# Cross attention: the probabilities turned by VectorE in 32x32 blocks and moved through DRAM

## Chip, cores and metric

The kernel is one program on 1 core of a Trainium2 chip. Its metric is the device time of one execution in microseconds, as a median of several runs. Engines are named as the profile names them: PE (TensorE), with PEld its weight loads, DVE (VectorE), ACT (ScalarE), POOL (GpSimd), SP (SyncE, which only issues DMAs here).

## The reference

The program computes a block of three layers over 64 sequences of 32 tokens of width 512, each layer added to its input: cross attention to 257 context rows of width 256, self attention, and a layer of experts. The change touches the first.

```python
def _L0_xattn_ref(x, z, Wq, Wkv, Wo):        # x (64, 32, 512) normalised, z (64, 257, 256)
    Q = (x @ Wq.T).reshape(B, xN, 16, 32)
    KV = (z @ Wkv.T).reshape(B, zN, 2, 16, 32)
    K, V = KV[:, :, 0], KV[:, :, 1]
    attn = jax.nn.softmax(jnp.einsum('bqhd,bkhd->bhqk', Q, K) * SCALE, axis=-1)
    O = jnp.einsum('bhqk,bkhd->bqhd', attn, V).reshape(B, xN, 512)
    return O @ Wo.T
```

## The kernel before

**Tiling.** 2048 tokens are 16 token tiles i of 128 tokens, each of which holds four samples (sequences) j of 32 tokens, so there are 64 samples s = 4i + j. The loop runs over pairs of tiles, with the first and the last pair written out. The key and value weights are absorbed: the queries of a tile are multiplied with Wk once (absorb_k), so that a sample's scores are QK times the raw context z, and the probabilities are multiplied with z first (gather_z, result U) and with Wv and Wo once per tile (values, project_o). A precise product is three matmuls in fp32r with operands split in a high and a low part (product, L49 to L54): ACT makes a high part by a cast, DVE the low part by a subtraction.

**One sample.** Rows are (head, token) pairs, in four groups m of 128 rows; columns are the 257 keys. PE makes the scores in four banks bank_s (scores, 24 matmuls), DVE takes two maxima (L696), ACT makes four exponentials into Pr with their sums (L596), DVE scales Pr by the reciprocal sums (L703, L707, L708). Keys 0 to 255 must then be brought onto the partitions for gather_z: PE turns the eight 128x128 blocks of Pr (turn_p, L412) into bank_pt, which are the banks 2 and 3 of bank_s; ACT casts them into PT_hi (L564) and DVE subtracts for PT_lo (L641), both out of PSUM. Key 256 has its own path (p_last, last_weights, last_rows, last_values).

**What prepares the next sample.** PE turns z (turn_z, L385), ACT casts it into zT_hi (L541) and DVE makes zT_lo (L628); ACT casts the sample's slice of QK (L558), DVE makes QK_lo (L633). POOL writes the last key's column (last_key, L742) and splits z, not turned, for gather_z (split_z: a small carrier instruction L748, the cast L749, the subtraction L751). SP loads the raw z of a sample four samples ahead (L142, 256 KB) and per tile eight small pieces for the last key (L355).

**Order.** It is written out by hand per engine, and each engine runs its list in order, with semaphores between them. PE in sample s: scores(s), gather_z(s-1), turn_z(s+1), then what belongs to the tile (absorb_k for j = 0 and 2, values at j = 0, project_o at j = 1, half of project_q at j = 2 and at j = 3), and turn_p(s) last. split_z(s) on POOL waits for the gather_z before it (pe_U), because it overwrites its buffer, and for DVE's QK_lo of the next sample (v_QK, L760).

Of the kernel before, what the change touches and what calls it, by code (L numbers as in the profile page):

```python
# [16 lines left out]
F32 = mybir.dt.float32  # L17
# [6 lines left out]
P = 128  # L24
# [60 lines left out]
def cross_attention(nc, x_in, ctx_in, Wq, Wkv, Wo, x_res, ident, vlast_dram, spare,  # L85
# [21 lines left out]
    with ExitStack() as ctx:  # L107
# [31 lines left out]
        z_got = [sem(f"z_got{j}") for j in range(BT)]  # L139

# [158 lines left out]
        (PT_hi, PT_lo) = held.parts(held.w13[1], 1, 2, C)  # L299
# [5 lines left out]
        OT_hi, OT_lo = held.parts(held.xT, 1, 2, P)  # L305
        carrier = sb("xa_carrier", [P, 1])
# [13 lines left out]
        g_L, g_Zh, g_Z = sem("g_L"), sem("g_Zh"), sem("g_Z")  # L320
# [18 lines left out]
        def step_of(i, u, j, more):  # L339

            if j % 2 == 0 and (more or u == 0):
                return 1 - u, j, 2 * (i + 1) + 2, BT * i + NQ + j + 2
            return None

        with nc.Block() as block:
            @block.sync
            def _(sp):
# [8 lines left out]

                def tile(i, u, first, last, more):
                    for j in range(BT):  # L360
                        s = BT * i + j
                        if not first:
                            sp.wait_ge(pe_T, s - BT + 1)
                            sp.wait_ge(g_Z, s - BT + 1)
                            load_z(sp, s, j)
                    if first:
# [4 lines left out]
                        sp.wait_ge(vl_put, 32)  # L371
                    last_values(i)
                    if first:
                        weights.load(sp)
                by_pair(sp, tile)

            @block.tensor
            def _(pe):
# [29 lines left out]
                def turn_p(s):  # L408
                    pe.wait_ge(v_N, s + 1)
# [11 lines left out]
                def scores(s, some):  # L421
# [3 lines left out]
                    for m in range(NQ):  # L425
                        if some and m >= 2:
                            pe.wait_ge(v_PT, 2 * s + m - 3)
# [5 lines left out]
                def gather_z(s):  # L433

                    pe.wait_ge(g_Z, s + 1)
                    pe.wait_ge(v_PT, 2 * s + 2)
                    need(pe, U_out, s)
                    for k in range(KL):
                        for c in range(CH):
                            mm = product(pe, bank_u[:, k],  # L440
                                         (zn_hi[:, c, k * P:(k + 1) * P], zn_lo[:, c, k * P:(k + 1) * P]),
                                         (PT_hi[:, c, :], PT_lo[:, c, :]), c == 0, c == CH - 1)
                    mm.then_inc(pe_U, 1)

# [7 lines left out]
                def values(i):  # L452

                    pe.wait_ge(U_out, BT * i + BT)
                    for m in range(NQ):
                        for part in range(KL):
                            for hh in range(4):
                                h = 4 * m + hh
                                mm = pe.matmul(bank_o[hh * HD:(hh + 1) * HD, m * P:(m + 1) * P],
                                               WvT[:, part, h * HD:(h + 1) * HD], U[:, part, h, :], start=False,  # L460
# [30 lines left out]
                def tile(i, u, first, last, more):  # L491
                    for j in range(BT):
# [4 lines left out]
                        if j == 0 and not first:  # L497
# [3 lines left out]
                        if first and j == 1:  # L501
# [3 lines left out]
                        if j == 0 and not first:  # L505
                            last_values(i - 1)
                        if j == 2 and not last:
                            need(pe, v_OP, i)
                            turn_x(pe, i + 2)
# [8 lines left out]
                        if j == 0 and not first:  # L518
                            values(i - 1)
                        if j == 1 and not first:  # L520
                            project_o(i - 1)
                        if j == 2 and more:
                            project_q(i + 2, 0)
                        if j == 3 and more:
                            project_q(i + 2, 1)
# [6 lines left out]
                gather_z(s_end - 1)  # L532
# [5 lines left out]
            def _(act):  # L538
# [22 lines left out]
                def pt_hi(s):  # L561
                    for c in range(CH):
                        act.wait_ge(pe_PT, 2 * s + c + 1)
# [1873 lines left out]
```

## Time and profile before

| | us |
|---|---|
| median of 3 runs (1493.66 to 1495.46) | 1495.41 |
| profiled execution, first to last instruction | 1492.9 |
| PE busy | 1434.5 (96%) |
| DVE busy | 1088.6 (73%) |
| ACT busy | 807.5 (54%) |
| POOL busy | 543.6 (36%) |
| TensorE clock granted, mean | 0.990 |

The profiled execution's own time was not kept beside its span; the span is 2.5 us under the median of the runs. In a row of a timeline the first number is the start in us from the span's start, the second the duration. A group of instructions gives their busy time and mean duration in ns, and, behind the bar, how long the engine idled just ahead of them and what ended that. Tile names are shortened by the profile: split and split_xT are parts of held buffers, xa_s is bank_s, xa_u the banks of gather_z, xa_z the bank of turn_z.

### The profile page before, as it was taken

What the parts mean: (1) busy time and instruction counts of PE and PEld (TensorE: products, weight loads), DVE (VectorE), ACT (ScalarE), POOL (GpSimd) and SP (SyncE); (2) the same over time, 40 slices, a digit from 0 to 9 for tenths busy, and PEclk for the clock granted to TensorE, in tenths of its full rate; (3) what the DMA queues carried; (4) which work ended last, traced back from release to release, by engine and by line L of the source; (5) the groups of instructions that cost most, each with busy time, mean ns of one, the idle gap of its engine ahead of it and who ended that gap; (6) DMA issues with size and microseconds to landing.
All of it is one profiled execution on the core that took longest, in us unless ns stands there. A gap on an engine that the chain in (4) does not pass through costs nothing. (4 is left out here: it accounts for less than half of the span.)

```text
span 1492.9 us, 39481 instructions
## 1 busy us (share of the span) xinstructions
PE 1434.5 (96%) x14944; PEld 1281.3 (86%) x14944; DVE 1088.6 (73%) x1945; ACT 807.5 (54%) x1525; POOL 543.6 (36%) x810
## 2 busy tenths in 40 slices
PE   7999999999999999998999998799999999999998
PEld 6888888988888888887778786698999999999997
DVE  3676777767777677776667686797887878787785
ACT  4666666666666666654434434345555545555452
POOL 1222222221222222224866876453333333333232
PEclk9999999999999999999999999899999999999999
DMA  6301101000001100100011014179877878787871
GB/s 239 125 28 31 30 22 29 29 22 29 22 28 28 29 28 23 30 9 1 31 38 38 32 38 155 57 220 314 281 263 247 286 253 267 262 279 238 292 256 44
DMA packets 130734, 174.11 MB, mean 117 GB/s; under 512 B 16953, under 2 KB 89337, under 8 KB 130626
## 3 DMA queue, kind: packets, MB, share of 16 engines
q1 hardware_dynamic: 120242, 145.56, 30.1%
q0 software_dynamic: 10384, 27.05, 5.0%
q8 instruction: 75, 1.23, 0.4%
q14 instruction: 33, 0.27, 0.1%
HBM read 157.18 MB, written 19.06 MB: 118 GB/s over the span
## 5 line engine op out<-in xcount | busy, mean ns | idle before, releaser
L2229 DVE TENSOR_TENSOR split<-raw,split 128x1024 fp32r<-128x1024 f32 x204 | 242.3, 1220 | 7.2 <-ACT split L2169 6.0
L52 PE MATMUL bank<-split_xT,split 128*128 128x256 f32 x768 | 216.5, 282 | 0.4 <-DVE split L2229 0.2
L54 PE MATMUL bank<-split_xT,split 128*128 128x256 f32 x768 | 215.4, 281 | 0.0
L53 PE MATMUL bank<-split_xT,split 128*128 128x256 f32 x768 | 215.4, 280 | 0.0
L2169 ACT CAST split<-raw 128x1024 fp32r<-128x1024 f32 x202 | 203.2, 1048 | 6.9 <-DMA raw<-in_L_ffn_W_dram 3.2
L596 ACT ACTIVATE Pr<-xa_s,nmax 128x257 f32<-128x257 f32 x256 | 118.7, 473 | 124.9 <-DVE nmax L696 124.8
L2189 ACT ACTIVATE sl<-bank 128x256 f32<-128x256 f32 x115 | 44.2, 384 | 240.8 <-PE bank L54 223.5
L52 PE MATMUL xa_s<-split,split 128*128 128x258 f32 x512 | 150.5, 294 | 1.9 <-DVE split L628 1.9
L52 PEld LDWEIGHTS bank<-split_xT,split 128*128 128x128 f32 x768 | 144.9, 189 | 7.0 <-issue 2.8
L53 PEld LDWEIGHTS bank<-split_xT,split 128*128 128x128 f32 x768 | 145.0, 189 | 3.1
L53 PE MATMUL xa_s<-split,split 128*128 128x258 f32 x512 | 145.6, 284 | 0.0
L54 PE MATMUL xa_s<-split,split 128*128 128x258 f32 x512 | 145.2, 284 | 0.0
L54 PEld LDWEIGHTS bank<-split_xT,split 128*128 128x128 f32 x768 | 144.8, 189 | 0.0
L641 DVE TENSOR_TENSOR split<-xa_s,split 128x512 fp32r<-128x512 f32 x128 | 82.6, 686 | 81.4 <-ACT split L564 80.1
L2313 POOL TENSOR_TENSOR e_carrier<-count 128x1 f32<-128x1 f32 x84 | 29.3, 349 | 306.8 <-DMA of_row<-slot_val 102.8
L748 POOL TENSOR_TENSOR xa_carrier<-mhalf 128x1 f32<-128x1 f32 x64 | 12.6, 197 | 285.2 <-DVE split L633 280.6
L696 DVE TENSOR_REDUCE nmax<-xa_s 128x2 f32<-128x514 f32 x128 | 87.9, 690 | 33.0 <-PE xa_s L54 32.1
L52 PE MATMUL bank<-split,a_hi 128*128 128x512 f32 x234 | 96.3, 412 | 7.0 <-DVE a_lo L2288 6.9
L52 PE MATMUL xa_u<-split,split_xT 128*128 128x512 f32 x256 | 102.3, 400 | 0.8 <-issue 0.8
L53 PE MATMUL xa_u<-split,split_xT 128*128 128x512 f32 x256 | 101.0, 395 | 0.0
L52 PEld LDWEIGHTS xa_s<-split,split 128*128 128x128 f32 x512 | 97.9, 191 | 3.6 <-DVE split L628 2.6
L54 PE MATMUL xa_u<-split,split_xT 128*128 128x512 f32 x256 | 101.0, 394 | 0.0
(317 smaller groups left out, 3915.1 us busy)
## 6 DMA issues: line engine op xcount, KB each, us to landing
raw<-in_L_ffn_W_dram SPq DMA_DIRECT2D x207, 512.0 KB
raw<-in_ctx_dram SPq DMA_DIRECT2D x64, 256.0 KB, 2.6
out_dram<-x_res SPq DMA_DIRECT2D x16, 256.0 KB
xs<-xn SPq DMA_DIRECT2D x16, 256.0 KB
x_res<-in_x_dram SPq DMA_DIRECT2D x1, 3584.0 KB, 18.7
VL<-v_last_rows SPq DMA_DIRECT2D x128, 2.0 KB, 1.5
raw_o<-in_L_xattn_Wo_dram SPq DMA_DIRECT2D x1, 1024.0 KB, 6.4
raw_q<-in_L_xattn_Wq_dram SPq DMA_DIRECT2D x1, 1024.0 KB, 9.5
```

What stands on the lines that cost most here:

```text
L52: pe.matmul(out, lh, rh, start=start, stop=False)
L53: pe.matmul(out, ll, rh, start=False, stop=False)
L54: return pe.matmul(out, lh, rl, start=False, stop=stop)
L596: act.activation(Pr[:, m, 0:NK], bank_s[:, m, 0:NK], ACT.Exp, bias=nmax[:, m:m + 1], scale=1.0, accum_out=rsum[:, m:m + 1]).then_inc(a_E, 1)
L641: dve.tensor_tensor(PT_lo[:, c, :], bank_pt[c], PT_hi[:, c, :].bitcast(F32), ALU.subtract).then_inc(v_PT, 1)
L696: dve.tensor_reduce(nmax[:, 2 * h:2 * h + 2], bank_s[:, 2 * h:2 * h + 2, 0:NK], AX_X, ALU.max, negate=True).then_inc(v_mx, 1)
L748: pool.tensor_tensor(carrier[:], mhalf[:], mhalf[:], ALU.add)
L2169: aW.done(act.copy(hi, raw), f"p{c}{q}")
L2189: aM.done(act.activation(sl[:, j % 2, :], bank_hg[j % 2][:, 0:ROWS], ACT.Silu), f"{pos}s{j}")
L2229: vW.done(dve.tensor_tensor(lo, raw, hi.bitcast(F32), ALU.subtract), f"p{c}{q}")
L2313: pool.tensor_tensor(carrier[:], count[:, 0:1], count[:, 0:1], ALU.add).then_inc(carried, 1)
```

## The change

**Turning.** Per sample DVE transposes Pr in 32x32 blocks (turn_blocks, two instructions of 128x512, reading keys in steps of four floats), into P_turned in SBUF. SP writes P_turned to a DRAM scratch (put, 512 KB) and reads it back in another partition order (meet, 512 pieces of 1 KB) into P_met. Then key 4i + b stands on partition 4i + b. Both buffers lie in the space of a weight slot that isn't used yet. ACT casts P_met into PT_hi and DVE subtracts for PT_lo, each as one instruction of 1024 elements out of SBUF. PE's turn_p, and with it the use of bank_s for turned probabilities, is left for the last sample alone, which has buffers of its own (PT_end, zn_end).

**Lag.** gather_z in sample s is that of s-2, not s-1. What is made from U moves with it by one sample: turn_last, last_values and values to j = 1, project_o to j = 2, turn_x to j = 3, one half of project_q to j = 3 and the other to j = 0 of the next tile. The scores of the next sample now wait for the exponentials bank by bank (a_E), not for PT_lo.

**POOL.** split_z is that of s-1, and no longer waits for v_QK.

**SP.** Per sample: write, load of z (three samples ahead), read back. The load of the output weights of the self attention is issued at the end of the stage.

```diff
@@ SP
+                def ask_z(s, j):
+                    sp.wait_ge(pe_T, s - BT + 1)
+                    sp.wait_ge(g_Z, s - BT + 1)
+                    sp.wait_ge(v_PTl, s - BT + 1)
+                    load_z(sp, s, j)
+
+                def put(s):
+                    sp.wait_ge(v_TP, CH * s + CH)
+                    sp.dma_start(put_dram, P_turned).then_inc(p_put, 16)
+
+                def meet(s):
+                    sp.wait_ge(p_put, 16 * s + 16)
+                    sp.dma_start(P_met.rearrange("p (r e) -> p r e", r=HEADS), met_dram).then_inc(p_met, 16)
...
+                        put(s)
...
+                            ask_z(s + BT - 1, (j + BT - 1) % BT)
+                        meet(s)
@@ PE
-                            pe.wait_ge(v_PT, 2 * s + m - 3)
+                        if some:
+                            pe.wait_ge(a_E, 4 * s + m - 3)
...
-                        if some:
-                            gather_z(s - 1)
+                        if not first or j >= 2:
+                            gather_met(s - 2)
...
-                        turn_p(s)
                 by_pair(pe, tile)
+                turn_p()
+                gather_met(s_end - 2)
@@ ACT
                 def pt_hi(s):
-                    for c in range(CH):
-                        act.wait_ge(pe_PT, 2 * s + c + 1)
-                        act.copy(PT_hi[:, c, :], bank_pt[c]).then_inc(a_PT, 1)
+                    act.wait_ge(p_met, 16 * s + 16)
+                    need(act, pe_U, s)
+                    act.copy(PT_hi.rearrange(by_head), P_met).then_inc(a_PT, 1)
...
+                        if j % 2 == 0 and not (first and j == 0):
+                            pt_hi(s - 1)
                         if not (last and j == BT - 1):
                             z_hi(s + 1)
+                        if j % 2 == 1:
+                            pt_hi(s - 1)
@@ DVE
+                def turn_blocks(s):
+                    need(dve, p_put, 16 * s)
+                    need(dve, p_met, 16 * s)
+                    dve.wait_ge(v_N, s + 1)
+                    for c in range(CH):
+                        dve.transpose(turned_blocks[:, c], Pr[:, :, c * P:(c + 1) * P].rearrange("p m (i b) -> p m b i", b=BT)
+                                      ).then_inc(v_TP, 1)
+
                 def pt_lo(s):
-                    for c in range(CH):
-                        dve.wait_ge(a_PT, 2 * s + c + 1)
-                        dve.tensor_tensor(PT_lo[:, c, :], bank_pt[c], PT_hi[:, c, :].bitcast(F32), ALU.subtract
-                                          ).then_inc(v_PT, 1)
+                    dve.wait_ge(a_PT, s + 1)
+                    dve.tensor_tensor(PT_lo.rearrange(by_head), P_met, PT_hi.rearrange(by_head).bitcast(F32), ALU.subtract
+                                      ).then_inc(v_PTl, 1)
...
                             z_lo(s + 1)
+                            turn_blocks(s)
+                        if not (first and j == 0):
+                            pt_lo(s - 1)
@@ POOL
-                            pool.wait_ge(v_QK, s + 2)
-                        split_z(s, j, i)
+                        if not (first and j == 0):
+                            split_z(s - 1, (j - 1) % BT, i if j else i - 1)
```

DVE, in the loop, sample j = 0 of a tile, from the small product for the last key to the end of the sample. Before (raw, split are SBUF buffers; L641 is PT_lo):

```order
L707 TENSOR_TENSOR p_last<-Pr,rinv 128x4 [waits v_PR,v_R]
L708 TENSOR_TENSOR Pr<-Pr,rinv 128x4x256
L669 COPY U<-xa_u 128x32x32 [waits pe_U]
L632 REGISTER_ALU
L633 TENSOR_TENSOR split_1<-QK,split_1 128x1024 [waits a_QKh]
L628 TENSOR_TENSOR split_0<-xa_z,split_0 128x2x256 [waits a_T]
L674 TENSOR_TENSOR split_xT<-xa_o,split_xT 128x512 [waits a_OT]
L640 ISA
L641 TENSOR_TENSOR split_1<-xa_s,split_1 128x512 [waits a_PT]
L640 REGISTER_ALU
L641 TENSOR_TENSOR split_1<-xa_s,split_1 128x512 [waits a_PT]
```

After (L697 turns the blocks, L702 is PT_lo of the sample before, L737 the copy of U):

```order
L775 TENSOR_TENSOR p_last<-Pr,rinv 128x4 [waits v_PR,v_R]
L776 TENSOR_TENSOR Pr<-Pr,rinv 128x4x256
L686 REGISTER_ALU
L687 TENSOR_TENSOR split_1<-QK,split_1 128x1024 [waits a_QKh]
L682 TENSOR_TENSOR split_0<-xa_z,split_0 128x2x256 [waits a_T]
L36 REGISTER_ALU
L697 STREAM_TRANSPOSE raw_2<-Pr 128x4x4x32 [waits v_N,p_met,p_put]
L697 STREAM_TRANSPOSE raw_2<-Pr 128x4x4x32
L702 TENSOR_TENSOR split_1<-raw_2,split_1 128x1024 [waits a_PT]
L736 REGISTER_ALU
L737 COPY U<-xa_u 128x32x32 [waits pe_U]
```

Two transposes and one subtraction out of SBUF stand where two subtractions out of PSUM stood, and the transposes wait for the DMAs of the sample before.

ACT, in the same sample, from its cast of QK on. Before (L541 is the z cast, L564 PT_hi):

```order
L558 CAST split_1<-QK 128x1024 [waits pe_S]
L540 REGISTER_ALU
L541 CAST split_0<-xa_z 128x2x256 [waits pe_T]
L550 REGISTER_ALU [waits v_QK]
L551 COPY QK<-xa_s 128x4x2x128 [waits pe_QK] x2
L568 CAST split_xT<-xa_o 128x512 [waits pe_O]
L564 CAST split_1<-xa_s 128x512 [waits pe_PT] x2
```

After (L603 is PT_hi of the sample before, L580 the z cast, L585 a half of the queries):

```order
L597 CAST split_1<-QK 128x1024 [waits pe_S]
L601 ISA
L603 CAST split_1<-raw_2 128x1024 [waits pe_U,p_met]
L579 REGISTER_ALU
L580 CAST split_0<-xa_z 128x2x256 [waits pe_T]
L589 REGISTER_ALU [waits v_QK]
L590 COPY QK<-xa_s 128x4x2x128 [waits pe_QK] x2
L583 REGISTER_ALU
L585 ACTIVATE raw_0<-xa_o 128x256 [waits pe_Q]
```

The cast of the probabilities moved from behind the copies of QK to ahead of the z cast, and waits for the read back.

POOL, one sample. Before:

```order
L742 COPY split_0<-zl_hi 128x2 [waits pe_S]
L742 COPY split_0<-zl_lo 128x2
L748 TENSOR_TENSOR xa_carrier<-mhalf 128x1 [waits pe_U,z_got2,v_QK]
L749 CAST split_xT<-raw_0 128x512
L751 TENSOR_TENSOR split_xT<-raw_0,split_xT 128x512 [waits g_Zh]
```

After (L821 is the carrier, L822 the cast, L824 the subtraction):

```order
L811 COPY split_0<-zl_hi 128x2 [waits pe_S]
L811 COPY split_0<-zl_lo 128x2
L821 TENSOR_TENSOR xa_carrier<-mhalf 128x1 [waits pe_U,z_got2]
L822 CAST split_xT<-raw_0 128x512
L824 TENSOR_TENSOR split_xT<-raw_0,split_xT 128x512 [waits g_Zh]
```

The wait for v_QK is gone; the one for pe_U stays.

## Rows read from the trace of the kernel before

**Rows 1.** The page's busy times: busy us, share of span, instructions.
```profile
PE 1434.5 (96%) x14944; PEld 1281.3 (86%) x14944; DVE 1088.6 (73%) x1945; ACT 807.5 (54%) x1525; POOL 543.6 (36%) x810
```

**Rows 2.** Windows, 100 to 600 us: length; busy PE, PEld, DVE, ACT, POOL; clock, DMA share, GB/s.
```profile
100.00:600.00 500.00, 497.14 (x4600) 446.97 (x4593) 356.08 (x618) 327.79 (x729) 122.29 (x260) 1.00 0.09 27
```

**Rows 3.** Timeline of DVE: start, us, engine, instruction; the scaling in one token tile.
```profile
299.95 1.22 DVE L708 TENSOR_TENSOR Pr<-Pr,rinv 128x1024 f32<-128x1024 f32 x1
...
340.34 1.22 DVE L708 TENSOR_TENSOR Pr<-Pr,rinv 128x1024 f32<-128x1024 f32 x1
```

**Rows 4.** Groups, 100 to 600 us, and timeline of PE around one sample's transposes.
```profile
L412 PEld LDWEIGHTS xa_s<-ident,Pr 128*128 128x128 f32 x400 | 44.4, 141 | 10.1 <-ACT QK L551 8.5
...
313.37 0.91 PEld L412 LDWEIGHTS xa_s<-ident,Pr 128*128 128x128 f32 x8
...
314.25 0.19 PEld L52 LDWEIGHTS xa_s<-split,split 128*128 128x128 f32 x1
```

**Rows 5.** Groups, 100 to 600 us: busy us, mean ns, idle before and releaser.
```profile
L54 PE MATMUL xa_u<-split,split_xT 128*128 128x512 f32 x196 | 77.3, 394 | 0.0
...
L633 DVE TENSOR_TENSOR split<-QK,split 128x1024 fp32r<-128x1024 f32 x50 | 60.9, 1217 | 0.0
...
L703 DVE RECIPROCAL rinv<-rsum 128x4 f32<-128x4 f32 x49 | 8.7, 178 | 36.0 <-ACT Pr L596 35.9
```

**Rows 6.** Timeline in the next stage: a block transpose on VectorE beside GpSimd.
```profile
803.09 0.71 DVE L1354 STREAM_TRANSPOSE Pt<-Pm 128x512 f32<-128x512 f32 x1
...
803.14 1.28 POOL L1549 TENSOR_TENSOR part_cos<-qraw,rope_t 128x512 f32<-128x512 f32 x1 [2.82 <-DVE Pm L1350]
...
803.73 0.42 DVE L1328 TENSOR_TENSOR latT_lo<-bank,latT_hi 128x256 fp32r<-128x256 f32 x1
```

**Rows 7.** Timeline of DVE and POOL in the last sample.
```profile
670.71 1.22 DVE L708 TENSOR_TENSOR Pr<-Pr,rinv 128x1024 f32<-128x1024 f32 x1
...
671.55 0.43 POOL L748 TENSOR_TENSOR xa_carrier<-mhalf 128x1 f32<-128x1 f32 x1 [4.55 <-PE xa_u L54]
...
671.97 0.59 DVE L657 CAST pl_hi<-p_last 128x16 fp32r<-128x16 f32 x1
...
672.61 1.29 POOL L751 TENSOR_TENSOR split_xT<-raw,split_xT 128x512 fp32r<-128x512 f32 x1
...
672.69 1.36 DVE L661 TENSOR_TENSOR p_rows<-pl_hi,head_mask 128x128 fp32r<-128x128 f32 x1
...
674.18 1.28 DVE L641 TENSOR_TENSOR split<-xa_s,split 128x512 fp32r<-128x512 f32 x2
```

**Rows 8.** Groups of ACT, 100 to 600 us.
```profile
L558 ACT CAST split<-QK 128x1024 fp32r<-128x1024 f32 x49 | 51.4, 1050 | 0.0
L551 ACT COPY QK<-xa_s 128x1024 f32<-128x1024 f32 x50 | 48.2, 1016 | 13.0 <-PE xa_s L404 13.0
...
L541 ACT CAST split<-xa_z 128x512 fp32r<-128x512 f32 x50 | 29.5, 589 | 25.5 <-PE xa_z L385 25.5
```

**Rows 9.** DMA issues: KB each, median us from issue to landing.
```profile
raw<-in_ctx_dram SPq DMA_DIRECT2D x64, 256.0 KB, 2.6
...
raw<-in_L_attn_wq_dram SPq DMA_DIRECT2D x1, 1024.0 KB, 5.8
...
x_res<-in_x_dram SPq DMA_DIRECT2D x1, 512.0 KB, 3.6
```

**Rows 10.** Timeline of DVE in the setup: a strided and a plain reduction.
```profile
15.13 0.37 DVE L279 TENSOR_REDUCE own_key<-ident 128x32 f32<-128x128 f32 x1
15.41 0.28 DVE L281 TENSOR_REDUCE head_mask<-ident 128x4 f32<-128x128 f32 x1
```

**Rows 11.** Groups of POOL, 100 to 600 us: the first instruction of the context's split.
```profile
L748 POOL TENSOR_TENSOR xa_carrier<-mhalf 128x1 f32<-128x1 f32 x50 | 9.6, 193 | 222.6 <-DVE split L633 222.6
```

**Rows 12.** Two lines of DVE in all 16 tiles: duration ns min/median/max.
```profile
L657 DVE CAST pl_hi<-p_last x16: 165/165/595, 73.5 to 672.0; 128x16 fp32r<-128x16 f32 x16
...
L661 DVE TENSOR_TENSOR p_rows<-pl_hi,head_mask x16: 284/285/1360, 73.8 to 672.7; 128x128 fp32r<-128x128 f32 x16
```

More of the change, by code:

```diff
@@ L370, in tile @@
                             sp.dma_start(vlast_dram[n], half[:].bitcast(F32)).then_inc(vl_put, 16)
-                        sp.wait_ge(vl_put, 32)
-                    last_values(i)
-                    if first:
                         weights.load(sp)
+                    for j in range(BT):
+                        s = BT * i + j
+                        if j == BT - 1:
+                            if first:
+                                sp.wait_ge(vl_put, 32)
+                            last_values(i)
+                        if last and j == BT - 1:
+                            return
+                        put(s)
+                        if last and j > 0:
+                            sp.wait_ge(v_PTl, s)
+                        elif not (first and j == 0):
+                            ask_z(s + BT - 1, (j + BT - 1) % BT)
+                        meet(s)
                 by_pair(sp, tile)
+                sp.wait_ge(a_PT, s_end - 1)
+                sp.wait_ge(v_PTl, s_end - 1)
+                weights.load_last(sp)
             @block.tensor
@@ L496, in tile @@
                         scores(s, some)
-                        if j == 0 and not first:
+                        if j == 1 and not first:
                             pe.wait_ge(a_Q, 2 * min(i + 2, n_tile) if isinstance(i, int) else 2 * i + 4)
@@ L600, in tile @@
                             qk_hi(s + 1, t, (j + 1) % BT, BT * i + (BT if j < BT - 1 else 2 * BT))
-                        if j == 2 and not last:
+                        if j == BT - 1 and not last:
                             x_out(act, i + 2)
+                        if j == 1 and not first:
+                            u_out(s - 2, BT - 1)
+                        if j % 2 == 0 and not (first and j == 0):
+                            pt_hi(s - 1)
                         if not (last and j == BT - 1):
                             z_hi(s + 1)
+                        if j % 2 == 1:
+                            pt_hi(s - 1)
                         if step is not None:
@@ L697, in tile @@
                                               negate=True).then_inc(v_mx, 1)
-                        if j == 0 and not first:
+                        if j == 1 and not first:
                             last_rows(i - 1)
@@ L709, in tile @@
                                           rinv[:].unsqueeze(2).to_broadcast([P, NQ, LAST]), ALU.mult).then_inc(v_N, 1)
-                        if j == 0 and not first:
-                            u_out(s - 1, BT - 1)
                         if not (last and j == BT - 1):
@@ L714, in tile @@
                             z_lo(s + 1)
+                            turn_blocks(s)
+                        if not (first and j == 0):
+                            pt_lo(s - 1)
+                        if j == 0 and not first:
+                            u_out(s - 2, BT - 2)
                         if j == 1:
@@ L718, in tile @@
                             statistics(dve, i + 2)
-                        if j == 0 and not first:
+                        if j == 1 and not first:
                             ot_lo(i - 1)
-                        if last and j == BT - 1:
+                        if j == 2 and not first:
+                            add_residual(i - 1)
+                        if j == BT - 1:
                             last_weights(i)
-                        pt_lo(s)
-                        if j == BT - 1 and not last:
-                            last_weights(i)
-                        if j == 1 and not first:
-                            add_residual(i - 1)
                 by_pair(dve, tile)
+                pt_end_lo()
                 last_rows(n_tile - 1)
```

117 lines of the change are left out of this document (74 added, 43 removed).

## The prediction

> **What bounds the kernel now.** I read the page's busy times first: PE is busy 96% of the span [rows 1]. A mean over stages doesn't price a change in one stage, so I took the stretch from 100 to 600 us, all of it inside the cross-attention loop: PE 497.1 of 500 us, DVE 356.1, ACT 327.8, POOL 122.3 [rows 2]. The loop is bound by PE's stream, not by a wait. Its beat comes from DVE's scaling of the probabilities: one such instruction per sample, four samples per token tile, five starts from 299.95 to 340.34 us, so 40.4 us per tile, 10.1 per sample [rows 3]. All estimates below are per tile and go by 16 tiles. They are made against this execution's span of 1492.9 us; the median of the runs is 1495.41, which is 2.5 us around the span, and I add the difference to the median.
>
> **What leaves PE.** The turning of the probabilities is 8 transposes per sample: from its first weight load at 313.37 us to the first one of the scores behind it at 314.25 are 0.88 us; ahead of them PE's weight path idled 10.1 us for 50 samples, 0.2 each [rows 4]. The idle has its reason in the shared banks (the transposes need ACT's copies of the absorbed queries out of the way), and the scores behind inherit that wait, so I count it as a gain only at best. PE would need 40.4 - 4 x 1.08 = 36.1 us per tile. If nothing else came to the end this would be worth 4.3 x 16 = 69 us. The other PE work is the same and only in another order; the moving operand is now read as four runs of 128 columns, which I cost at nothing, since no row shows a price for that.
>
> **What DVE gets.** Out: two subtractions from PSUM, 1.28 us as a pair, the last row of [rows 7]. In: one of 1024 elements out of SBUF, like those of L633, 1.22 us [rows 5], and two block transposes. The trace has such transposes in the next stage, 128x512 in 0.71 us, with the next instruction 0.64 us after its start [rows 6]. That is 1.22 - 1.28 + 1.28 = 1.22 us more per sample, 4.9 per tile. DVE's busy time per tile is now 356.1 / 500 x 40.4 = 28.8, so 33.7. What it can't fill is the wait between the second maximum and the end of the four exponentials (36.0 us of idle before L703 in the stretch, 2.9 per tile [rows 5]): 36.6. So DVE comes to where PE is, 36.1, before any disturbance. The cover is gone: from here each delay on DVE is a delay of the loop.
>
> **The wait that POOL loses.** Today POOL's split of the context starts only when DVE's QK_lo is done; it waited 222.6 us for that in the stretch [rows 11]. The change drops this wait, and POOL starts when the product over the context (gather_z) is done. The trace has one sample where this happened already, the last: POOL's run went from 671.55 to 673.90, and beside it DVE's cast of 16 elements took 0.59 us and the product of 128 took 1.36 [rows 7], where the other fifteen of each took 0.17 and 0.28 [rows 12]. Both ended within 0.15 us of POOL's instruction. A DVE instruction with its inputs in SBUF that starts beside one of POOL's ends when POOL's does, and POOL's first, started under L708, ended with L708. That sample lost 0.43 + 1.07 = 1.5 us on DVE. In the loop the run meets L708, QK_lo's subtraction (L633) and the new subtraction. If it arrives under L708 it waits through to the end of the next one and then lies beside the z subtraction and the transposes, costing about 0.2 (2.1 us of run against 0.7 + 1.28); if DVE is late, it comes first and pushes L708 and L633 by up to 1.5. Even samples have more DVE work ahead (U's copy, the last rows' weights), so I take 1.5 there and 0.3 in odd ones: 3.6 per tile, bounds 0.8 and 6. DVE's tile: 36.6 + 3.6 = 40.2.
>
> **The new round trip.** Each sample now writes 512 KB to DRAM and reads it back, and SP issues the read only after the write has landed, DVE's next transposes wait for the read, ACT's copy too. Nearest rows: 256 KB landed in 2.6 us after issue, 512 KB in 3.6 and 1024 KB in 5.8, all of them reads [rows 9]. I take 3.6 for each way and 0.2 for SP to wake: a round trip RT of 7.4 us; below, 2 x 2.6 = 5.2, since half the bytes land so; above, 2 x 5.8 = 11.6. The Trainium skill, SBUF — State Buffer, section "The DMA setup-cost knee", gives about 2 us plus the bytes over 436 GB/s, which by estimate is 3.2 us each way and a trip of 6.6; the rows show 3.6 for this size, so the sum doesn't use the rule; with it the chain below would be 36.0 and the total some 10 us less, about 1495. Two chains follow. In odd samples: transposes end, RT, next transposes (1.28). In even samples ACT copies the fetched block (1.05, as L558 takes for the same size) ahead of the z cast (0.59 [rows 8]), DVE's z subtraction (0.6) follows and only then the transposes: RT + 1.05 + 0.59 + 0.6 + 1.28. Two of each: 4 RT + 9.6 = 39.2 per tile. Longer than PE's 36.1 and DVE's undisturbed 36.6, shorter than 40.2, and close enough that the two collide in some samples: in even ones ACT's copies of QK (about 1.0 each [rows 8]) come behind the fetched block, and PE's next scores wait for them. I take 0.6 per tile for that, between 0 and 2.
>
> **Sum.** 40.2 + 0.6 = 40.8 against 40.4: 0.4 x 16 = +6.4 us. The lag of two samples moves one more product over the context (12 matmuls of 0.39 us, overlapping [rows 5]) from the first tile, where PE then waits for DVE, to the end: 4.7 at most, and since they overlap I take 3. The late load of the output weights, 1024 KB, lands 5.8 us after issue [rows 9] and is first used over 20 us later: nothing. Together +9.4: **1505 us**.
>
> **A rule against the change.** DVE's new transposes read SBUF in steps of four floats (16 bytes). The trace has two reductions of 128 elements over the same tile, one in steps of 32 floats, 0.37 us, one without a step, 0.28 us [rows 10]; the first also writes 32 values for 4. If the whole 0.09 is due to the step, 512 elements cost 0.35 more, two per sample, 2.8 per tile. The rows don't settle if a step of four is enough. The Trainium skill, Advanced Engine Details and Errata, section "Memory Cachelines", says that SBUF is read in lines of 16 bytes and that an access to another line each time costs extra; by that rule the price would be paid here in full.
>
> **Rivals.**
> (a) POOL doesn't disturb, or the trip is shorter, and the loop gets faster. For it: PE and DVE alone need 36.1 and 36.6; all of POOL's run may fall beside the transposes, which it doesn't stretch (0.71 us with a product of POOL's beside it from 803.14 on [rows 6]). With RT at 6.8, 0.3 less each way, the chain is 36.8, and some collision of the three chains, put at 2, makes it 38.9: -1.5 x 16 + 3 = -21, **1474**, between 1462 and 1488. It decides when the stretch of DVE is under 0.5 us per sample and RT under 7.2.
> (b) The trip is the bound. The reads come in 512 pieces of 1 KB instead of 128 of 2 KB, and each shares the queue with a 256 KB load of z. From RT = 7.7 on the chain is over 40.4 alone; at 8.4 it is 43.2, so +2.8 x 16 = +45 and 3: **1543**; at 8.0 it is 1517.
> (c) The steps cost as above: of the 2.8 some hides the collisions, I leave 1.8: 42.6, +2.2 x 16 + 3 = +38, **1533**, with half of it about 1519.
> (d) Gains and losses cancel, within 3 us of 1495.4; that is a part of my forecast's own width (stretch 0.7 rather than 0.9).
>
> **Chances.** Forecast with its width, 1492 to 1517: 0.46, of which 0.12 lie within 0.2% of before (3 us, about what a measurement of this kernel tells from no change). (a) 0.22, (b) 0.19, (c) 0.13. The range 1475 to 1543 leaves out half of (a) and the worst of (b) and (c). Faster 0.23, same 0.12, slower 0.65.
>
> **What would show it.** In the loop: PE's busy share under 95% with a clock still at 1.0, DVE's at about 85% or more; DVE's scaling, QK_lo or cast groups with a maximum of 2 to 2.5 us, where L633 now has a mean of 1.217 [rows 5]; the transposes at 0.71 us (right) or about 1.05 (c); the write and the read landing in 3.6 us (right) or over 4 (b); ACT idle for the fetched block in even samples only; five scaling starts 40.8 us apart. I am wrong if the fetched block is always there before ACT asks and DVE still has idle time between the exponentials and the next maxima: then PE sets the beat, at 36 to 38.

## The result

The changed kernel takes 1554.69 us (median of 4 runs, 1548.65 to 1556.93) against 1494.54 us in the same session: a ratio of 1.0391, 95% interval 1.0369 to 1.0412. It is 60 us slower. I had said slower, by 10 us, with 1543 as the upper end. The profiled execution after spans 1554.5 us.

The time from 100 to 600 us after, with the columns of [rows 2]:

```profile
100.00:600.00 500.00, 450.58 (x3908) 391.22 (x3907) 442.84 (x629) 296.19 (x634) 164.46 (x244) 0.98 0.37 122
```

PE fell from 497.1 to 450.6 us of 500, DVE rose from 356.1 to 442.8. The loop is no longer PE's. The scaling of the probabilities comes once per sample, so its starts give the time per sample. Its row has the shortest, median and longest duration in ns and the first and last of its 64 starts:

```profile
L776 DVE TENSOR_TENSOR Pr<-Pr,rinv x64: 1211/1218/2331, 37.7 to 722.5; 128x1024 f32<-128x1024 f32 x64
```

722.5 less 37.7 over 63 steps is 10.87 us per sample; before it was (670.7 - 37.5)/63 = 10.05. That is 51.6 us of the 61.6 between the spans. The next stage starts 22.6 us behind the last scaling, before 16.8 (+5.8), and takes 809.4 us, before 805.4 (+4.0); 0.2 are at the start.

DVE's costliest groups, 100 to 600 us: busy us, mean ns of one, idle just ahead and who ended it:

```profile
L697 DVE STREAM_TRANSPOSE raw<-Pr 128x512 f32<-128x512 f32 x93 | 97.4, 1085 | 0.0
L687 DVE TENSOR_TENSOR split<-QK,split 128x1024 fp32r<-128x1024 f32 x46 | 72.2, 1569 | 0.0
L776 DVE TENSOR_TENSOR Pr<-Pr,rinv 128x1024 f32<-128x1024 f32 x46 | 61.9, 1345 | 0.0
L764 DVE TENSOR_REDUCE nmax<-xa_s 128x2 f32<-128x514 f32 x94 | 61.0, 684 | 8.7 <-PE xa_s L54 7.6 <-issue 1.1
...
L775 DVE TENSOR_TENSOR p_last<-Pr,rinv 128x4 f32<-128x4 f32 x46 | 13.7, 298 | 1.6
...
L771 DVE RECIPROCAL rinv<-rsum 128x4 f32<-128x4 f32 x46 | 8.1, 176 | 44.4 <-ACT Pr L641 44.4
```

Three readings. The transposes take 1.085 us each, where I had 0.71. QK_lo's subtraction (L687), the scaling (L776) and the small product for the last key (L775) have means above the 1.217, 1.22 and 0.16 us that they take alone; this is what I call the stretch, DVE's instructions made longer by POOL's run beside them. And DVE's time is full: 442.84 busy is 9.63 us per sample, the wait for the exponentials (44.4 over 46 samples) 0.97, the wait for scores (8.7) 0.19, together 10.79 of 10.87.

The trip is shorter than I took, 6.5 us instead of 7.2 (DMA issues: KB each, median us to landing):

```profile
turned_probabilities<-raw SPq DMA_DIRECT2D x63, 512.0 KB, 2.6
raw<-turned_probabilities SPq DMA_DIRECT2D x63, 512.0 KB, 3.9
```

And this is the stretch in the making, the timeline after at one even sample (start, us, engine, instruction, idle before it):

```profile
300.55 0.19 POOL L821 TENSOR_TENSOR xa_carrier<-mhalf 128x1 f32<-128x1 f32 x1 [2.54 <-PE xa_u L54]
...
300.68 0.61 POOL L822 CAST split_xT<-raw 128x512 fp32r<-128x512 f32 x1
...
301.23 1.21 DVE L776 TENSOR_TENSOR Pr<-Pr,rinv 128x1024 f32<-128x1024 f32 x1
301.37 2.20 POOL L824 TENSOR_TENSOR split_xT<-raw,split_xT 128x512 fp32r<-128x512 f32 x1
302.36 2.29 DVE L687 TENSOR_TENSOR split<-QK,split 128x1024 fp32r<-128x1024 f32 x1
```

POOL's subtraction, 1.29 us alone [rows 7], came 0.14 us behind DVE's scaling and ended only 1.1 us behind the scaling's end; DVE's next, which reads two tiles of SBUF too, ended 1.1 us behind POOL's. The two took turns, each for a whole instruction. The Trainium skill, SBUF — State Buffer, section "Who interferes with whom", describes the port pair that VectorE and GpSimd share as an exclusive lock held for the instruction. The trace agrees with that.

### The profile page after: what moved, and what is told of

Its sections match the earlier page's. It is cut to its first block and busy times, and to the rows that moved or that the text cites. A ratio compares the mean times of both kernels' runs of the same rounds, so it can differ in the third digit from the quotient of the medians.

```text
span 1554.5 us, 38819 instructions
## 1 busy us (share of the span) xinstructions
PE 1424.3 (92%) x14440; PEld 1257.2 (81%) x14440; DVE 1234.5 (79%) x2008; ACT 795.6 (51%) x1462; POOL 610.4 (39%) x810
## 5 line engine op out<-in xcount | busy, mean ns | idle before, releaser
L641 ACT ACTIVATE Pr<-xa_s,nmax 128x257 f32<-128x257 f32 x256 | 118.3, 474 | 235.4 <-DVE nmax L764 235.4
L52 PE MATMUL xa_s<-split,split 128*128 128x258 f32 x512 | 160.9, 314 | 65.5 <-ACT QK L590 48.8
L52 PEld LDWEIGHTS xa_s<-split,split 128*128 128x128 f32 x512 | 107.3, 210 | 80.0 <-issue 51.2
L53 PE MATMUL xa_s<-split,split 128*128 128x258 f32 x512 | 155.1, 303 | 0.0
L54 PE MATMUL xa_s<-split,split 128*128 128x258 f32 x512 | 154.8, 302 | 0.0
L697 DVE STREAM_TRANSPOSE raw<-Pr 128x512 f32<-128x512 f32 x126 | 132.0, 1085 | 0.0
L811 POOL CAST split<-zl_hi 128x2 fp32r (+1 forms) x64 | 12.9, 202 | 269.8 <-PE xa_s L54 268.8
L52 PE MATMUL xa_u<-split,split_xT 128*128 128x512 f32 x256 | 105.5, 412 | 3.3 <-DVE split L702 1.8
L54 PEld LDWEIGHTS xa_s<-split,split 128*128 128x128 f32 x512 | 107.6, 210 | 0.0
L53 PEld LDWEIGHTS xa_s<-split,split 128*128 128x128 f32 x512 | 107.2, 209 | 0.0
L824 POOL TENSOR_TENSOR split_xT<-raw,split_xT 128x512 fp32r<-128x512 f32 x64 | 103.1, 1611 | 5.1
L53 PE MATMUL xa_u<-split,split_xT 128*128 128x512 f32 x256 | 102.0, 399 | 0.0
```

What stands on the lines that cost most here:

```text
L52: pe.matmul(out, lh, rh, start=start, stop=False)
L53: pe.matmul(out, ll, rh, start=False, stop=False)
L54: return pe.matmul(out, lh, rl, start=False, stop=stop)
L641: act.activation(Pr[:, m, 0:NK], bank_s[:, m, 0:NK], ACT.Exp, bias=nmax[:, m:m + 1], scale=1.0, accum_out=rsum[:, m:m + 1]).then_inc(a_E, 1)
L697: dve.transpose(turned_blocks[:, c], Pr[:, :, c * P:(c + 1) * P].rearrange("p m (i b) -> p m b i", b=BT)).then_inc(v_TP, 1)
L824: pool.tensor_tensor(lo[:], z_in[j], hi[:].bitcast(F32), ALU.subtract).then_inc(g_Z, 1)
```

## The experiments

Three things on DVE or around it were in dispute: the price of the steps, POOL's stretch and the trip. The kernels switch them one by one and in pairs. (QK_lo's subtraction, the scaling and the small product are L686, L775 and L774 in e9, e10 and e12.) In the table "loop" is the last start of the scaling less the first, over 63, from each one's profiled execution. The kernel before had medians of 1494.5 to 1497.4 us in the sessions, so differences between two kernels are those of their ratios to it, times 1495 us.

**The steps alone.** The transposes read 32 neighbouring keys at a time; the keys get another order, which leaves the work the same and the output not the reference's.

```diff
-dve.transpose(turned_blocks[:, c], Pr[:, :, c * P:(c + 1) * P].rearrange("p m (i b) -> p m b i", b=BT)
+dve.transpose(turned_blocks[:, c], Pr[:, :, c * P:(c + 1) * P].rearrange("p m (b i) -> p m b i", b=BT)
```

> The changed kernel with one edit: VectorE's block transposes read the keys one after another instead of in steps of four floats. The keys then come out in another order than the context's, so the output is not the reference's; every instruction, size and DMA is as before. Theory (the loop is bound by VectorE, and 0.37 us of each of the 126 transposes is the price of the step): transposes at 0.71 us, loop period down by most of 0.74 us per sample, time 1505 to 1520 us. Rival (the round trip through DRAM with ScalarE's copy behind it sets the period, VectorE's time lies beside it): transposes at 0.71 us, but the time stays at 1545 to 1555. Second rival (not the step, the order of blocks or a slower way for strided 4-dimensional patterns costs): transposes stay at 1.08 us, time 1555.

Measured: 1500.56 us, ratio 1.0026 (1.0006 to 1.0046) to the kernel before, 55 us less than the changed kernel and 4 us below the range that I expected. All 126 transposes, now and in the changed kernel:

```profile
L697 DVE STREAM_TRANSPOSE raw<-Pr x126: 660/684/704, 40.4 to 661.9; 128x512 f32<-128x512 f32 x126
```
```profile
L697 DVE STREAM_TRANSPOSE raw<-Pr x126: 1039/1076/1162, 40.5 to 716.4; 128x512 f32<-128x512 f32 x126
```

The step costs 0.39 to 0.40 us per transpose, 0.80 per sample. With it went nearly all of POOL's stretch too, which nobody had taken away (L687's mean fell from 1.569 to 1.298 us): so 1.3 us of DVE's time went per sample, and the loop got 0.87 shorter. That the rest was kept by another chain, e6 and e9 show below.

**POOL's wait alone, in the changed and in the old kernel.** `pool.wait_ge(v_QK, s + 2)` is put back into the changed kernel (e2), and taken out of the kernel before (e4).

> The changed kernel with the old wait of GpSimd for VectorE's QK_lo back in front of the split of the context. Theory (GpSimd's run in front of VectorE's scaling and QK_lo stretches them by 0.6 us per sample in the mean, on the path): no scaling or QK_lo over 1.25 us, time down by 25 to 38 us, 1517 to 1530. Rival (the stretch lies in a wait that VectorE would have anyway, for the fetched block or the exponentials): durations back, time within 8 us of 1555.

> The kernel before with GpSimd's wait for QK_lo taken away, as the change does. Theory (GpSimd arrives 3.1 us after the scores, when VectorE's scaling is under way; it then waits for the scaling, gets its small first instruction in at the boundary, and waits again for QK_lo, so VectorE loses next to nothing in samples where it is on time, and 1.3 us in those where it is late): time 1494 to 1505. Rival (each overlap costs as in the changed kernel, 0.6 us per sample on the path): 1520 to 1530.

Measured: e2 1538.76 us (1.0287, 1.0252 to 1.0323), 16 us less than the changed kernel; L687 and the scaling at most 1.225 us. The durations came out as expected, the time didn't: it lies between the theory (1517 to 1530) and the rival (within 8 us of 1555). e4 1496.77 us (1.0000, 0.9986 to 1.0014): the same change costs nothing in the old kernel. It does stretch DVE there, whose busy time in the 500 us rises from 356.1 to 365.4 us, but DVE has room for it.

**Both, with the reference's order.** Reads without a step and POOL's wait; to put the keys right, PE turns z through a permutation matrix in place of the identity.

```diff
-pe.transpose(bank_z[:, at:at + P], z_in[j][:, c, k * P:(k + 1) * P], ident[:])
+pe.transpose(bank_z[:, at:at + P], z_in[j][:, c, k * P:(k + 1) * P], order_of)
```

> Both edits together, and with the right order of keys: the context is turned by TensorE through a permutation matrix instead of the identity, so that the scores' columns stand in the order that transposes without a step need. Same instruction counts in the loop. Theory (both costs sit on VectorE's path and add up until TensorE's stream or the round trip takes over): loop period about 9.9 us per sample or less, time 1480 to 1500, near the kernel before. Rival (round trip sets the period): 1535 or more.

Measured: 1502.82 us, 1.0043 (1.0025 to 1.0062), 3 us above the range of the theory. Once the steps are gone, POOL's wait gains nothing over e1 (e5 also changes the order of the keys; e8 and e13 below differ by POOL's wait alone and agree). What is late now shows in e1's timeline, in an even sample:

```profile
319.58 1.04 ACT L603 CAST split<-raw 128x1024 fp32r<-128x1024 f32 x1 [1.29 <-DMA raw<-turned_probabilities]
...
320.53 0.58 ACT L580 CAST split<-xa_z 128x512 fp32r<-128x512 f32 x1
...
321.00 1.93 ACT L590 COPY QK<-xa_s 128x1024 f32<-128x1024 f32 x2
321.14 0.69 DVE L682 TENSOR_TENSOR split<-xa_z,split 128x512 fp32r<-128x512 f32 x1 [1.11 <-ACT split L580]
...
323.26 0.38 PE L52 MATMUL xa_s<-split,split 128*128 128x258 f32 x1 [1.42 <-ACT QK L590]
```

ACT waits 1.29 us for the fetched block; the z cast and the two copies of QK stand behind it, DVE waits 1.11 us for the one and PE's scores 1.42 us for the other.

**The order on ACT (e6, e7).** On top of e1, ACT casts z ahead of the fetched block in the even samples too (e6), and the two copies of QK as well (e7).

```diff
-                        if j % 2 == 0 and not (first and j == 0):
-                            pt_hi(s - 1)
                         if not (last and j == BT - 1):
                             z_hi(s + 1)
-                        if j % 2 == 1:
+                        if not (first and j == 0):
                             pt_hi(s - 1)
```

> The changed kernel with step-one reads (keys in another order, as in e1_step_one), and ACT casts z before it takes the fetched block in the even samples too. Theory: in e1 the even samples are set by the trip through DRAM, ACT waits 1.3 us for the fetched block and the z cast stands behind it; taking the z cast out from behind it saves most of that, about 1 us in two samples of four, 32 us in all at most, half of it if the copies of QK behind the block become the next to be late: 1470 to 1485 us. Rival (the trip is hidden, something else bounds e1): stays at 1500 us.

> As e6, and ACT takes the fetched block behind its two copies of QK as well. Theory (what stands behind the awaited block on ACT is what PE waits for): nothing that PE needs soon is behind the trip any more, the loop comes near PE's own 9.0 us per sample: 1440 to 1465 us. Rival: DVE's subtraction waits for ACT's copy, which now ends 2 us later, and DVE comes late to the next maxima: no better than e6, or 1500 us and more.

Measured: e6 1481.04 us, 0.9913 (0.9885 to 0.9941); e7 1484.68 us, 0.9935 (0.9914 to 0.9956). The theory held for the z cast (17 us less than e1) and missed for the rest. In e7 DVE waits longer for the four exponentials (50.6 us before the reciprocal against 41.8) and its busy time rises to 439.9 us of 500 against 427.0; PE's is the same, 481.2 against 480.7. Most of DVE's 12.9 us is POOL's stretch come back, in e6 and in e7 (busy us, mean ns):

```profile
L685 DVE TENSOR_TENSOR split<-QK,split 128x1024 fp32r<-128x1024 f32 x52 | 64.8, 1246 | 0.0
L685 DVE TENSOR_TENSOR split<-QK,split 128x1024 fp32r<-128x1024 f32 x52 | 78.3, 1506 | 0.0
```

In the samples j = 2 POOL's run starts 0.68 us ahead of DVE's scaling in e7, in e6 at the same moment. So the order on ACT can't be judged apart from POOL's phase, and the two kernels' intervals overlap.

**The trip taken away (e9, e10).** Nothing goes to DRAM; the transposes write two buffers by turns and ACT and DVE read them there. Keys and heads stay in the blocks' order, so the output isn't the reference's. e9 is e1 without the trip, e10 the changed kernel without it.

```diff
-                        put(s)
-                        meet(s)
...
-                    need(dve, p_put, 16 * s)
-                    need(dve, p_met, 16 * s)
+                    need(dve, a_PT, s - 1)
+                    need(dve, v_PTl, s - 1)
...
-                        dve.transpose(turned_blocks[:, c],
+                        dve.transpose(turned_blocks[j % 2][:, c],
...
-                    act.wait_ge(p_met, 16 * s + 16)
+                    act.wait_ge(v_TP, CH * s + CH)
```

> As e1 (step-one reads, ACT in its first order), but nothing is written to DRAM or read back: ACT and DVE read the blocks where the transposes put them, in two buffers by turns, so the keys and heads stay in the blocks' order and the output is not the reference's. Prices the whole trip, waits and traffic. Theory: with trip and steps gone PE's 36.1 us per tile and DVE's 36.6 are left, some 9.1 us per sample, 57 us below e1: about 1445 us. Rival (the trip is hidden in e1): 1500 us. Rest of the program behind the loop: if the traffic costs clock there, it gets shorter by some us as well; if not, it stays at 807 us.

> The changed kernel as it is (reads in steps of four floats), without the trip, as in e9. Theory (the steps make DVE the bound, 9.55 us busy and 0.73 of waiting for the exponentials per sample): 10.3 us per sample against 10.87, 36 us below the changed kernel: about 1519 us, and the difference to e9 is larger than the 47 us that the steps cost on DVE's busy time. Rival (the trip is the bound and the steps only lengthen its chain): under 1490 us.

Measured: e9 1467.77 us, 0.9818 (0.9795 to 0.984); e10 1555.14 us, 1.0397 (1.0375 to 1.0419). Without the trip the changed kernel takes what it takes with it. My theory (DVE is the bound) was right and its number, 1519, wrong: I had taken DVE's stretch from the changed kernel and its wait for the exponentials from the one before. Both are larger here:

```profile
100.00:600.00 500.00, 436.16 (x3838) 375.47 (x3837) 451.20 (x617) 286.55 (x624) 151.65 (x238) 1.00 0.09 24
```
```profile
L686 DVE TENSOR_TENSOR split<-QK,split 128x1024 fp32r<-128x1024 f32 x46 | 80.7, 1755 | 0.0
...
L774 DVE TENSOR_TENSOR p_last<-Pr,rinv 128x4 f32<-128x4 f32 x45 | 25.9, 575 | 1.6
...
L770 DVE RECIPROCAL rinv<-rsum 128x4 f32<-128x4 f32 x45 | 8.0, 178 | 44.9 <-ACT Pr L640 44.9
```

The stretch grew to (1.755 - 1.217) + (0.575 - 0.162) = 0.95 us per sample, DVE is busy 451.2 us and waits 44.9 for the exponentials: 496 of 500. The clock is 1.00 here and the DMA share 0.09, in the changed kernel 0.98 and 0.37, at the same time per sample. That is a net result, not a trip without effect. By the scaling's starts, as means over samples 8 to 59, the changed kernel takes 0.5 and 0.3 us longer than e10 in the samples j = 0 and 2, where ACT waits for the fetched block, and 0.5 and 1.0 us less in j = 1 and 3 (over these samples it is 0.17 us per sample shorter, which the first and last ones make up). In j = 3 POOL's run is 0.68 us ahead of the scaling in e10, and with it or up to 0.7 behind it in the changed kernel, where L687 stays at 1.22 us. Such a sample of e10:

```profile
327.64 0.19 POOL L820 TENSOR_TENSOR xa_carrier<-mhalf 128x1 f32<-128x1 f32 x1 [2.53 <-PE xa_u L54]
...
328.32 1.22 DVE L775 TENSOR_TENSOR Pr<-Pr,rinv 128x1024 f32<-128x1024 f32 x1
328.46 2.20 POOL L823 TENSOR_TENSOR split_xT<-raw,split_xT 128x512 fp32r<-128x512 f32 x1
329.45 2.29 DVE L686 TENSOR_TENSOR split<-QK,split 128x1024 fp32r<-128x1024 f32 x1
```

So the trip delays the even samples, and the stretch that appears without it takes about the same time back; that the two come out equal is chance.

e9 missed its 1445 by 23 us:

```profile
100.00:600.00 500.00, 490.10 (x4456) 429.77 (x4455) 432.39 (x709) 339.64 (x722) 206.51 (x277) 1.00 0.10 29
```

PE is the bound again, at 98%, but with 9.56 us per sample, not 9.03. The rest of the program takes 805.9 us, as in e5 with its traffic (805.5), so the traffic in the loop costs nothing there.

**Steps without trip and stretch (e12).** e10 with POOL's wait put back.

> The changed kernel with its reads in steps of four floats, no trip through DRAM (as e10, the keys and heads in the blocks' order) and POOL's wait for QK_lo put back. In e10 DVE was busy 9.80 us per sample, 0.95 of it the stretch beside POOL, and waited 1.0 for the exponentials. Theory (DVE's busy time is the bound and POOL's stretch a part of it): 9.8 us per sample, 63 times 0.95 less than e10: about 1495 us; and against e2 (1539 us, with the trip) some 44 us that the trip costs as soon as POOL doesn't stretch DVE. Rival (the stretch is filled by other waits, DVE isn't the bound): as e2, 1535 to 1540 us.

Measured: 1501.42 us, 1.0042 (1.0025 to 1.0059), 6 us over the theory's 1495 and far from the rival. From 100 to 600 us:

```profile
100.00:600.00 500.00, 469.03 (x4218) 408.12 (x4215) 447.31 (x672) 316.63 (x685) 123.47 (x262) 1.00 0.09 27
```

DVE is busy 447.3 us, at 10.09 us per sample 9.03, and waits 46.7 for the exponentials (0.94). So, as net costs, the stretch costs 53 us where the trip isn't there (e10 to e12), and only 16 where it is (changed kernel to e2); the trip costs 37 us where POOL doesn't stretch (e12 to e2), 31 with reads without a step (e9 to e1), and nothing in the changed kernel. The trip's cost stands in the even samples: from e12 to e2 the samples j = 0 and 2 get 1.48 and 0.56 us longer, j = 1 and 3 0.11 and 0.01; from e9 to e1 it is 1.08 and 0.58 against nothing. Both together cost 52 (e12 to the changed kernel). Together:

| kernel | reads in steps of four | POOL free | trip | us | loop |
|---|---|---|---|---|---|
| changed | yes | yes | yes | 1554.69 | 10.87 |
| e10 | yes | yes | no | 1555.14 | 10.86 |
| e2 | yes | no | yes | 1538.76 | 10.67 |
| e12 | yes | no | no | 1501.42 | 10.09 |
| e1 | no | yes | yes | 1500.56 | 10.00 |
| e6, z cast first | no | yes | yes | 1481.04 | 9.78 |
| e9 | no | yes | no | 1467.77 | 9.56 |

**Which steps cost (e11).** Each sample's two transposes are cut in four of 256 elements: without a step (L698), in steps of four over the same shape (L699), in steps of two (L700), without a step over the shape of L700 (L701). The keys get another order.

```diff
+dve.transpose(one[:, 0:2], keys[:, 0:2].rearrange("p m (b i) -> p m b i", b=BT))
+dve.transpose(one[:, 2:4], keys[:, 2:4].rearrange("p m (i b) -> p m b i", b=BT)).then_inc(v_TP, 1)
+dve.transpose(two[:, 0:4, 0:2], others[:, :, 0:P // 2].rearrange("p m (i b) -> p m b i", b=2))
+dve.transpose(two[:, 0:4, 2:4], others[:, :, P // 2:P].rearrange("p m (b i) -> p m b i", b=2)).then_inc(v_TP, 1)
```

> The changed kernel with each sample's two transposes of 512 elements cut in four of 256: one reads without a step, one in steps of four floats (16 bytes), one in steps of two (8 bytes), and one without a step over the other halves. The keys get another order. Theory (each new line of 16 bytes costs): without a step about 0.35 us, in steps of four 0.2 more (half of the 0.40 that 512 elements cost), in steps of two half of that, 0.1 more. Rival (any step costs the same): steps of two also 0.2 more. Other rival (each row of 32 costs by where it starts): no difference between two and none.

Measured, a single run of 1526.57 us whose durations are what matters:

```profile
L698 DVE STREAM_TRANSPOSE raw<-Pr x63: 427/434/445, 40.3 to 688.7; 128x256 f32<-128x256 f32 x63
```
```profile
L699 DVE STREAM_TRANSPOSE raw<-Pr x63: 584/601/627, 40.7 to 689.1; 128x256 f32<-128x256 f32 x63
```
```profile
L700 DVE STREAM_TRANSPOSE raw<-Pr x63: 390/401/416, 41.2 to 689.6; 128x256 f32<-128x256 f32 x63
```
```profile
L701 DVE STREAM_TRANSPOSE raw<-Pr x63: 390/401/415, 41.5 to 689.9; 128x256 f32<-128x256 f32 x63
```

Steps of four floats cost 0.167 us over 256 elements against the same shape without a step, steps of two nothing at all. Of the theory the price of steps of four held (0.2), and its 0.1 for steps of two fell, as did the first rival. The second rival named the outcome; where a row starts was not varied, so its reason isn't tested. The Trainium skill, Advanced Engine Details and Errata, section "Memory Cachelines", says that at least two hits on a 16-byte line are needed to hide the access; steps of two floats hit each line twice, steps of four once. The trace agrees with that.

**A version that beats both (e8, e13).** e6 with the keys in the reference's order, as in e5, everything computed; e13 has POOL's wait as well.

> Step-one reads and the z cast ahead of the fetched block, as in e6, with the keys in the reference's order: z is turned through a permutation matrix in place of the identity, which costs PE nothing. Everything that the reference asks for is computed. Theory: what e6 gave, 1481 to 1485 us, a ratio of 0.990 to 0.994 to the kernel before. Rival (the copies of the order matrix and the waits on it cost what e5 seemed to cost over e1, 2 us): 1483 to 1487 us.

> As e8_z_first_ordered, and POOL waits for QK_lo again before it splits the context. Theory (with step-one reads POOL's run falls where DVE isn't stretched, DVE's scaling has a maximum of 1.24 us in e6): no difference to e8_z_first_ordered beyond 2 us. Rival (the wait puts POOL's run later, and the product over the context with it): some 5 to 10 us more.

Measured: e8 1486.60 us against 1494.60, ratio 0.9954 (0.9938 to 0.9970); e13 1487.17 us, 0.9952 (0.9935 to 0.9970). Both are faster than the kernel before by about 0.5%, and 65 us faster than the changed kernel; POOL's wait makes no difference, as expected. e8's time is over the 1481 to 1485 us of the theory and within the rival's 1483 to 1487; its loop is e6's, 9.78 us per sample, so no cost of the order shows in the loop. e8 from 100 to 600 us:

```profile
100.00:600.00 500.00, 481.57 (x4401) 421.58 (x4400) 425.96 (x695) 334.59 (x707) 203.82 (x270) 1.00 0.41 135
```

PE is back at 96% with 9.78 us per sample, 0.27 less than before. Its loop is 17.3 us shorter than before. The next stage starts 21.9 us behind the last scaling, not 16.8, and takes 1.5 us more, which leaves 10.6 between the two profiled executions and 8.0 between the medians.

## Why the prediction was wrong

The direction and the engine were right (DVE becomes the bound, "each delay on DVE is a delay of the loop"); the size was off by a factor of six. The step that failed is the third of these, the transposes. By the prediction's own steps, per sample:

1. **What leaves PE**, 1.08 us: too much. e9, where PE is the bound, has 9.56 us and not 9.03. The 0.2 that I counted as a gain at best didn't go, it stands elsewhere: in e9 PE's weight path waits at the scores, the query projection, the values and absorb_k, 28.6 us in the 500, 0.55 per sample, against 12.7, 0.26, before (8.5 of them at the transposes that left). I had these waits fall by 0.2 and they rose by 0.29, which would make up 0.49 of the missing 0.53. The product over the context, whose operand in four runs I cost at nothing, takes 394 ns as before. In the changed kernel, with PE at 90%, it didn't set the beat.
2. **What DVE gets**, had the transposes cost what [rows 6] show: right. My 33.7 us per tile are 8.43 per sample; e9 measures 432.39/500 x 9.56 = 8.27.
3. **The transposes**, 0.71 us each: this is the step that failed. They take 1.085, 0.75 per sample more, 47 us over 63 samples. The mechanism was in my text and so was nearly its price: 0.35 per transpose from [rows 10], and the row that gave 0.71 [rows 6] read its tile without a step. Yet I kept it out of the sum, gave it 0.13, and in rival (c) itself let 1.0 of its 2.8 per tile go because "some hides the collisions". Here DVE is full, 10.79 us of 10.87, and nothing hid it; without the steps the kernel is 55 us faster (e1). The forecast's own sum with the measured 3.0 per tile is 40.8 + 3.0 = 43.8, so +3.4 x 16 + 3 over 1495.4: 1553. That this comes so near is partly luck: the other errors, below, cancel.
4. **POOL**, 0.90 us per sample: right in kind, 0.61 in the changed kernel ((1.569 - 1.217) + (1.345 - 1.219) + (0.298 - 0.162)), 0.95 in e10. What I didn't see is that it depends on the other terms. POOL stretches DVE where its run starts ahead of the scaling, and that happens when DVE is late. In the samples j = 0 it starts 0.68 us ahead in the changed kernel, and L687 takes 2.29 us; with DVE 0.8 us faster (e1) it starts 0.4 to 0.8 behind, and L687 takes 1.22. So taking the steps away takes nearly all of the stretch with it, 1.3 us of DVE's time together.
5. **The wait for the exponentials**, 0.73: it grew to 0.97, and 0.19 for the scores came with it. I had carried it over unchanged from the kernel before, and no run varies it alone, so why it grew isn't shown.
6. **The trip**, 7.4 us: 6.7 with SP's 0.2, shorter, since the write took 2.6; the read in pieces of 1 KB took 3.9. Rival (b), the trip as the bound, fell: the changed kernel is no faster without it (e10). Yet the chain that I drew for the even samples is where the trip costs, 31 to 37 us as soon as POOL doesn't stretch DVE, and moving one instruction of ACT out of it gave 17 back (e6).
7. **Lag and end**, +3: measured +5.8 at the end of the loop, where ACT waits for the last fetched block and two products over the context follow:

```profile
724.10 1.05 ACT L603 CAST split<-raw 128x1024 fp32r<-128x1024 f32 x1 [2.36 <-DMA raw<-turned_probabilities]
```

   The later load I had put at nothing; the rest of the program took 4.0 us more. In the experiments the rest ranges from 805.5 to 811.7 us, the highest in e10, which has no traffic, so it isn't the traffic. The same 8908 matmuls keep PE busy there for 777.2 us in the changed kernel and 777.4 in e10, 772.5 before, at a granted clock of 0.977 and 0.976 against 0.985. So most of the 4.0 goes with a lower granted clock, though not strictly (e6 has 0.989 and 807.4 us); why it was lower no run shows.

DVE's account closes: 10.05 as predicted, and 0.75 for the transposes, 0.24 and 0.19 for the waits, less 0.29 of stretch and 0.16 of base, is 10.78, where the trace has 10.79. The waits' +0.43 and the -0.45 behind them cancel, which nothing in the prediction foresaw. The 0.15 per sample for collisions has no row of its own; 0.08 of the 10.87 are unaccounted. A slip in rival (a), 38.9 for 36.8 + 2, moves its 1474 by under 2 us. The loop accounts for 45 us of the 50 that I was short, the end and the rest for 7; the offset between span and median, 2.5 us before and 0.2 after, takes 2.3 back.

## What to carry to other kernels

Price an operation at its own access pattern, not by its name: the same transpose took 0.68 us or 1.08 by the step of its input, and on the engine that sets the beat such a term belongs in the sum undiscounted. When a change leaves several costs near the bound, switch them in pairs: here stretch and trip cost 53 and 37 us each where the other is absent and 52 together, so that undoing one alone gained 16 and nothing. Keep an awaited transfer's first reader behind everything on its engine that others wait for, as long as that doesn't make its own reader late.

## What the runs showed of the hardware

- A block transpose of 128x512 in float32 takes 0.684 us with neighbouring elements and 1.076 in steps of 16 bytes; over 256 elements 0.401 with steps of 8 bytes and 0.401 without.
- 512 KB of SBUF landed in DRAM 2.6 us after issue, and came back in pieces of 1 KB in 3.9 (medians of 63).
- In these traces VectorE and GpSimd alternate by whole instructions when both read SBUF and VectorE reads two tiles of it, and who starts first decides who pays: 2.20 and 2.29 us in the changed kernel for what takes 1.29 and 1.22 alone. Block transposes, which read one tile, aren't stretched beside GpSimd (the last two rows). In e6 GpSimd's cast starts 0.07 us behind VectorE's subtraction and takes 1.61 us instead of 0.61, and VectorE loses nothing:

```profile
305.10 1.22 DVE L685 TENSOR_TENSOR split<-QK,split 128x1024 fp32r<-128x1024 f32 x1
...
305.17 1.61 POOL L820 CAST split_xT<-raw 128x512 fp32r<-128x512 f32 x1
...
306.84 1.29 DVE L695 STREAM_TRANSPOSE raw<-Pr 128x512 f32<-128x512 f32 x2
306.87 1.28 POOL L822 TENSOR_TENSOR split_xT<-raw,split_xT 128x512 fp32r<-128x512 f32 x1
```
